# One level of Strassen's scheme for the gate, up and down products of a two-stage fp32 block

## The reference

```python
# stage 0, per batch element b: a dense layer plus a sum over signs
sign = 2 * mask - 1                                  # mask is 0/1, 8 x 1024 x 1024
x = x + (x @ W.T + bias + (x @ sign) * coeff[b])
# stage 1: gated feed-forward layer, F = 2752, with low-rank adapters (rank 16, one of 16 for each b)
gate = x @ W_gate.T + lora(x, A_gate, B_gate)
up   = x @ W_up.T   + lora(x, A_up, B_up)
act  = silu(gate) * up
x = x + (act @ W_down.T + lora(act, A_down, B_down))
# lora(v, A, B) = ((v @ A[i].T) @ B[i].T) * 0.5
```

## Time and profile before

| | |
|---|---|
| median of 3 runs | 1733.05 us (1732.14 to 1736.02) |
| span of the profiled execution | 1731.7 us; what lies around it is not recorded, the median is 1.35 us above it |
| busy: PE, VectorE, ScalarE, POOL | 98%, 49%, 36%, 5% |
| matmuls | 8192 |
| moved by DMA | 216.86 MB, mean 125 GB/s |

### The profile page before, as it was taken

The page is one execution under the profiler, slowest core; times in us unless marked ns, Lnnn a source line. Parts: engine busy times, 40 slices in busy tenths (PEclk is TensorE's granted clock), DMA queues, the critical chain, the costliest instruction groups (busy, mean ns, idle before and its releaser), DMA issues.

```text
span 1731.7 us, 23473 instructions
## 1 busy us (share of the span) xinstructions
PE 1702.4 (98%) x8192; PEld 1437.0 (83%) x8192; DVE 841.2 (49%) x1178; ACT 631.8 (36%) x938; POOL 80.2 (5%) x158
## 2 busy tenths in 40 slices
PE   7899999999999999999999999999999999999998
PEld 7788888888988888888897888888889788888887
DVE  8644334336954334433784433443478443333335
ACT  7433233235733223322663322332366332232222
POOL 1001001001000100100100010010010001000000
PEclk9999999999999999999999999999999999999999
DMA  8625234325742423423573242342366324223222
GB/s 306 175 85 127 90 115 122 99 86 154 245 136 90 130 88 114 124 97 102 171 234 118 88 127 85 121 119 97 96 197 222 110 87 123 97 86 107 90 71 77
DMA packets 66212, 216.86 MB, mean 125 GB/s; under 512 B 9360, under 2 KB 9488, under 8 KB 66128
## 3 DMA queue, kind: packets, MB, share of 16 engines
q1 hardware_dynamic: 54704, 188.97, 34.3%
q0 software_dynamic: 6816, 18.49, 4.9%
q10 hardware_dynamic: 4608, 8.39, 1.3%
HBM read 207.43 MB, written 8.39 MB: 125 GB/s over the span
## 4 chain that ended last, share of the span: by engine, by line
PE 95%; DMA 2%; DVE 1%; issue 1%; ACT 1%; SPq 0%; ACTq 0%; DVEq 0%
PE gate_ps L900 12%; PE gate_ps L904 12%; PE gate_ps L901 12%; PE up_ps L904 9%; PE up_ps L900 9%; PE up_ps L901 9%; PE down_ps L900 9%; PE down_ps L901 9%; PE down_ps L904 9%; DMA raw<-in_mask 2%; PE up_ps L903 1%; PE gate_ps L903 1%; PE td_ps L1008 1%; PE td_ps L1010 1%; PE ta_ps L952 1%
## 5 line engine op out<-in xcount | busy, mean ns | idle before, releaser
L631 DVE TENSOR_TENSOR lo<-raw,hi 128x1024 fp32r<-128x1024 f32 (+2 forms) x368 | 403.1, 1096 | 54.6 <-ACT hi L376 49.9
L376 ACT ACTIVATE hi<-raw 128x1024 fp32r<-128x1024 f32 (+1 forms) x336 | 342.5, 1019 | 218.7 <-PE down_ps L904 152.9
L900 PE MATMUL down_ps<-acth,hi 128*128 128x512 f32 x672 | 262.2, 390 | 0.3 <-DVE stage L634 0.3
L904 PE MATMUL gate_ps<-x1h,lo 128*128 128x512 f32 x672 | 262.3, 390 | 0.0
L904 PE MATMUL up_ps<-x1h,lo 128*128 128x512 f32 x672 | 262.3, 390 | 0.0
L900 PE MATMUL up_ps<-x1h,hi 128*128 128x512 f32 x672 | 262.0, 390 | 0.0
L900 PE MATMUL gate_ps<-x1h,hi 128*128 128x512 f32 x672 | 261.9, 390 | 0.0
L901 PE MATMUL down_ps<-actl,hi 128*128 128x512 f32 x672 | 261.9, 390 | 0.0
L901 PE MATMUL up_ps<-x1l,hi 128*128 128x512 f32 x672 | 261.8, 390 | 0.0
L901 PE MATMUL gate_ps<-x1l,hi 128*128 128x512 f32 x672 | 261.8, 390 | 0.0
L904 PE MATMUL down_ps<-acth,lo 128*128 128x512 f32 x672 | 261.6, 389 | 0.0
(11 more groups left out here) (92 smaller groups left out, 1959.8 us busy)
## 6 DMA issues: line engine op xcount, KB each, us to landing
raw<-in_wgu SPq DMA_DIRECT2D x168, 512.0 KB, 3.3
raw<-in_mask SPq DMA_DIRECT2D x64, 512.0 KB, 3.6
raw<-in_wd SPq DMA_DIRECT2D x64, 512.0 KB, 3.7
w_in<-in_w SPq DMA_DIRECT2D x32, 512.0 KB, 4.9
raw<-in_wd SPq DMA_DIRECT2D x32, 384.0 KB, 4.1
out<-stage ACTq DMA_DIRECT2D x32, 256.0 KB, 2.5
b_in<-in_b_gu POOLq DMA_DIRECT2D x48, 128.0 KB, 5.3
x_in<-in_x POOLq DMA_DIRECT2D x24, 256.0 KB, 2.9
```

The source lines that it names most:

```text
L376: return nc.scalar.activation(o, i, ACT.Copy)
L631: return nc.vector.tensor_tensor(o, a, b, ALU.subtract)
L900: mm(dst, hi[:, u, w], vh, start=first, stop=False)
L904: end = mm(dst, lo[:, u, w], vh, start=False, stop=last)
```

## The change

Each of the three large products A B is cut into quarters and done by Winograd's form of Strassen's scheme: 7 products of quarter size for 8, at the price of sums of quarters ahead of and behind them. The quarters of A are weight tiles (for gate and up, the rows of the two matrices are paired so that a11 and a12 belong to the gate and a21 and a22 to the up matrix, as the host lays them out; for down, they are pairs of output tiles), the columns of B are two halves of 512 tokens each, and the inner dimension is halved.

- The batch is worked in two blocks s of 1024 tokens (four elements), each in two halves of 512 columns.
- Stage 0 is done for the whole batch first: 64 chunks in a row. x1 is written to DRAM (`x1_scratch`) by POOL.
- For each s, x1 is read back through six buffers `fx`, the sums t1 to t4 of its quarters are made (`form_make`) and seven operands of four k tiles each are split and kept in SBUF (`op_b`). The order of reading, making and splitting is the list `FORM`; the first pair of tiles is done in the order of `FIRST_PRODUCTS` while the operands form, with the adapter products `ta` in between.
- For each of 21 pairs of gate and up tiles: four weight quarters of 128 x 512 are loaded, four sums s1 to s4 made (`make_first`, `make_second`), seven tiles split, seven products p1 to p7 made in three PSUM banks. Later products go on in the bank of earlier ones, so ScalarE or VectorE first takes out what the bank holds (`copied`, `c_made`). The half-filled last pair uses four products (`FUSED`).
- The activations are split, their sums t1 to t4 made, split too and stored in DRAM (`operand_scratch`) as seven operands for each pair of feature tiles, 512 KB each, by POOL.
- Down runs in 5 segments of two k pairs; the 14 operand tiles of a segment (7.34 MB) are read back by POOL (`load_operand`) into one of two sets in `op_d`; for each of 4 pairs hp of output tiles 7 products of 6 matmuls are made, and VectorE adds each at once to `acc` (`add_down`), which starts as x1 read back from DRAM. The last one and a half feature tiles of down (`left`) are done as before.
- The loops are unrolled: every engine has straight code, and one counter (`pe_done`) tells how far TensorE has got.

The core of the diff (the lines that go are those of the functions printed above):

```diff
-BLOCKS, PAIR = 4, 2
-T = PAIR * S
+BLOCKS, HALVES = 2, 2
+N = HALVES * S
...
+PRODUCTS = ["p1", "p5", "p6", "p3", "p7", "p2", "p4"]
+FIRST_PRODUCTS = ["p1", "p2", "p5", "p6", "p3", "p7", "p4"]
+FUSED = ["q1", "q2", "q3", "q4"]
+WEIGHT = {"p1": "a11", "p5": "s1", "p6": "s2", "p3": "s4", "p7": "s3", "p2": "a12", "p4": "a22",
+          "q1": "a11", "q2": "a12", "q3": "sum", "q4": "neg"}
...
+MOVING = {"p1": "b11", "p5": "t1", "p6": "t2", "p3": "b22", "p7": "t3", "p2": "b21", "p4": "t4",
+          "q1": "b11", "q2": "b21", "q3": "b22", "q4": "t2"}
...
+def pe_order():
+    order = [("s", m) for m in range(2 * len(first_stage_order()))]
+    for s in range(BLOCKS):
+        order += [("g", s, 0, "p1"), ("g", s, 0, "p2")] + [("ta", s, k) for k in range(KQ)]
+        order += [("g", s, 0, "p5")] + [("ta", s, k) for k in range(KQ, HT)]
+        order += [("g", s, 0, u) for u in FIRST_PRODUCTS[3:]]
+        for f in range(1, PAIRS):
+            order += [("g", s, f, u) for u in PRODUCTS[:4]] + [("td", s, f - 1)]
+            order += [("g", s, f, u) for u in PRODUCTS[4:]]
+        order += [("g", s, PAIRS, u) for u in FUSED[:2]] + [("td", s, PAIRS - 1)]
+        order += [("g", s, PAIRS, u) for u in FUSED[2:]]
+        for seg in range(SEGS):
+            for hp in range(HP):
+                order += [("d", s, seg, hp, u) for u in PRODUCTS]
+                if seg == 0 and hp == 0:
+                    order += [("td", s, PAIRS)]
+        order += [("l", s, h) for h in range(HT)]
+    return order
...
+    x1_d = nc.dram_tensor("x1_scratch", (BLOCKS, HT, HALVES, P, N), f32, kind="Internal").ap()
+    ops_d = nc.dram_tensor("operand_scratch", (BLOCKS, KP, 7, P, 2 * N), f32r, kind="Internal").ap()
+    a20_d = nc.dram_tensor("act_scratch", (BLOCKS, HALVES, P, 2 * N), f32r, kind="Internal").ap()
...
+        FORM = ([("b11", k) for k in range(KQ)] + [("b21", k) for k in range(KQ)] + [("t1", k) for k in range(KQ)]
+                + [(n, k) for k in range(KQ) for n in ("b22", "t3", "t2", "t4")])
...
+            def fx_dma(s, name):
+                n = fx_index[s, name]
+                if n >= FX_RING:
+                    old_s, old = fx_list[n - FX_RING]
+                    if old[0] == "t1b":
+                        sp.wait_ge(form_t, form_t_count(old_s, "t1", old[1]))
+                    else:
+                        sp.wait_ge(form_l, form_count(old_s, *old))
+                o, h = next((o, h) for e, o, h in fx_loads if e == name)
+                sp.dma_start(fx_ap(s, name), x1_d[s, o, h, :, :]).then_inc(fx_loaded[n % FX_RING], 16)
...
+            def load_operand(s, seg, u):
+                name = MOVING[u]
+                for kp in range(SEGK):
+                    at_op = opd_at(seg, name, kp, 0)
+                    pool.dma_start(op_d[:, at_op:at_op + 2, :].rearrange("p a n -> p (a n)"),
+                                   ops_d[s, seg * SEGK + kp, STORED[name], :, :]
+                                   ).then_inc(opd_loaded[opd_sem(seg, name, kp)], 16)
...
+                for i, count in enumerate(stores_upto((s, KP, "b11"))):
+                    pool.wait_ge(ot_stored[i], 16 * count)
+                pool.wait_ge(pe_done, done["g", s, PAIRS - 1, "p4"])
+                for u in PRODUCTS[:4]:
+                    load_operand(s, 0, u)
+                pool.wait_ge(a21_l, HALVES * (s + 1))
+                load_acc(s, 0)
+                load_acc(s, 1)
+                pool.wait_ge(pe_done, done["g", s, PAIRS, "q4"])
+                for u in PRODUCTS[4:]:
+                    load_operand(s, 0, u)
+                for h in range(2, HT):
+                    load_acc(s, h)
+                for half in range(HALVES):
+                    pool.dma_start(a20[:, 2 * half:2 * half + 2, :].rearrange("p a n -> p (a n)"), a20_d[s, half, :, :]
+                                   ).then_inc(a20_loaded, 16)
+                for u in PRODUCTS:
+                    load_operand(s, 1, u)
...
+                for seg in range(2, SEGS):
+                    for u in PRODUCTS:
+                        pool.wait_ge(pe_done, done["d", s, seg - 2, HP - 1, u])
+                        load_operand(s, seg, u)
+                pool.wait_ge(pe_done, done["d", s, SEGS - 2, HP - 1, PRODUCTS[-1]])
...
+            def form_make(s, name, k):
+                def loaded(e):
+                    n = fx_index[s, (e, k)]
+                    dve.wait_ge(fx_loaded[n % FX_RING], 16 * (n // FX_RING + 1))
+                loaded(name)
+                own_ap = fx_ap(s, (name, k))
+                if name == "t1":
+                    loaded("t1b")
+                    end = sub(own_ap, own_ap, fx_ap(s, ("t1b", k)))
+                elif name == "t3":
+                    loaded("b22")
+                    end = sub(own_ap, fx_ap(s, ("b22", k)), own_ap)
+                elif name == "t2":
+                    dve.wait_ge(form_t, form_t_count(s, "t3", k))
+                    end = add(own_ap, fx_ap(s, ("t3", k)), own_ap)
+                else:
+                    dve.wait_ge(form_t, form_t_count(s, "t2", k))
+                    end = sub(own_ap, own_ap, fx_ap(s, ("t2", k)))
+                end.then_inc(form_t, 1)
+            def form_lo(s, name, k):
+                dve.wait_ge(form_h, form_count(s, name, k))
+                sub(op_b[:, op_at(name, k, 1), :], fx_ap(s, (name, k)), op_b[:, op_at(name, k, 0), :]
+                    ).then_inc(form_l, 1)
...
+            def make_second(g):
+                dve.wait_ge(s_made, plan.made[g, "s3"])
+                dve.wait_ge(lo_ready, at[(*g, "p1")] + 1)
+                sub(raw_ap(g, "a11"), raw_ap(g, "s1"), raw_ap(g, "a11")).then_inc(s_made, 1)
+                dve.wait_ge(s_made, plan.made[g, "s2"])
+                if plan.entry_after[g, "s4"]:
+                    dve.wait_ge(lo_ready, plan.entry_after[g, "s4"])
+                sub(raw_ap(g, "s4"), raw_in(g, "a12"), raw_ap(g, "a11")).then_inc(s_made, 1)
...
+                elif u == "p3":
+                    dve.wait_ge(pe_done, done[key])
+                    dve.wait_ge(copied, copy_count(s, f, "p6"))
+                    if f:
+                        dve.wait_ge(a_made, a_count(s, f - 1, 0))
+                    else:
+                        dve.wait_ge(t_ready, 4 * (s + 1))
+                    add(g2[:, :], u2c[:, :], y_ps[:, :]).then_inc(c_made, 1)
+                elif u == "p7":
+                    dve.wait_ge(pe_done, done[key])
+                    dve.wait_ge(copied, copy_count(s, f, "p5"))
+                    add(u2[:, :], x_ps[:, :], p5c[:, :]).then_inc(c_made, 1)
+                    dve.wait_ge(silu_made, silu_count(s, f, 1))
+                    dve.wait_ge(c_made, c_count(s, f, "c22"))
+                    if f > 1 and f % 2 == 0:
+                        dve.wait_ge(ot_l, ot_index[s, kp - 1, "t3"] + 1)
+                    mult(a32[:, 1 + f % 2, :], g2[:, :], u2[:, :]).then_inc(a_made, 1)
+                    if f > 1 and f % 2 == 0:
+                        for name, src in (("t2", t_sum[:, :]), ("t4", a32[:, 0, :])):
+                            operand_lo((s, kp - 1, name), src)
+                elif u == ("p2" if f else "p4"):
+                    dve.wait_ge(pe_done, done[key])
+                    dve.wait_ge(copied, copy_count(s, f, "p1"))
+                    add(g1[:, :], p1c[:, :], z_ps[:, :]).then_inc(c_made, 1)
+                    operand_lo((s, kp, ("b12", "b22")[f % 2]), a32[:, 1 + f % 2, :])
+                if u == "p4":
+                    dve.wait_ge(pe_done, done[key])
+                    dve.wait_ge(silu_made, silu_count(s, f, 0))
+                    dve.wait_ge(c_made, c_count(s, f, "c11"))
+                    if f % 2:
+                        dve.wait_ge(tm, tm_count(s, kp, "t1"))
+                    elif f:
+                        dve.wait_ge(ot_l, ot_index[s, kp - 1, "t4"] + 1)
+                    mult(a32[:, 0, :], g1[:, :], x_ps[:, :]).then_inc(a_made, 1)
+                    operand_lo((s, kp, ("b11", "b21")[f % 2]), a32[:, 0, :])
+                    dve.wait_ge(a_made, a_count(s, f, 0))
+                    if f % 2:
+                        dve.wait_ge(ot_l, ot_index[s, kp, "b21"] + 1)
+                        sub(a32[:, 1, :], a32[:, 2, :], a32[:, 1, :]).then_inc(tm, 1)
+                        sub(t_sum[:, :], a32[:, 2, :], t_sum[:, :]).then_inc(tm, 1)
+                        dve.wait_ge(tm, tm_count(s, kp, "t2"))
+                        sub(a32[:, 0, :], a32[:, 0, :], t_sum[:, :]).then_inc(tm, 1)
+                    elif f < PAIRS - 1:
+                        sub(t_sum[:, :], a32[:, 1, :], a32[:, 0, :]).then_inc(tm, 1)
+                    lora_b(s, f + 1)
...
+            def add_down(key):
+                _, s, seg, hp, u = key
+                g = (s * SEGS + seg) * HP + hp
+                x_ps, y_ps, z_ps = ps[3 * (g % 2)], ps[3 * (g % 2) + 1], ps[3 * (g % 2) + 2]
+                bank = {"p5": y_ps, "p3": y_ps, "p2": z_ps}.get(u, x_ps)
```

(99 more changed lines are left out.)

1735 lines of the change are left out of this document (943 added, 792 removed).

## The result

Median 1717.6 us (1715.0 to 1718.8, four runs) against 1733.9 of the kernel before (1732.1 to 1736.0, four runs): ratio 0.9904, 95% interval 0.9892 to 0.9915, 1.0% faster. The forecast was 1673 us, 3.5% faster. The saving of matmul work came as counted; the new stops cost 44 us more than my sum.

A forecast was written before the change was run, and what follows sets the result against it. TensorE, busy 1702.4 of 1731.7 us, was taken to bound the kernel. After the change 1534.1 us of matmul work plus 138 us of stalls gave a 1672 us span, so 1673 us measured; forecast 1650 to 1695, wider range 1630 to 1722.

The forecast's parts named there:

- Work saved: Whole kernel: PE work falls by 156.1 us to 1534.1 us, with 7502 matmuls left.
- Stage 0: 64 chunks in a row at the start: 4 us lost (bounds 0 and 15).
- four signs of being wrong: Gate pairs over 21.7 us; down group over 11; op_d landing over 40 after issue; stage 0 ending past 215.
- Operands and first pair: First gate and up pair of each half, operands formed from x1: 62 us lost together (bounds 30 and 90).
- Start of down: Start of down, twice: PE waits for operands being loaded, 24 us for both (bounds 10 and 50).
- Down, steady: the coupling: Steady down: products wait for late VectorE adds, 0.5 us in each of 40 groups, 20 us (bounds 0 and 60).
- End: End of the kernel: two adds, issue and a 512 KB store, 5.5 us.
- paced by adds or clock: Rival, 1713 us, chance 0.17: down groups lose 1.5 us instead of 0.5, or slower-clock matmuls after stops cost 43.
- Slower through POOL's queue: Rival, 1765 us, chance 0.1: in down the operands come too slowly through POOL's queue.
- Better hidden: Rival, 1631 us, chance 0.18: neighbouring k reads overlap (62 becomes 42), slack in down absorbs late adds (20 becomes 0).

The follow-up runs named there:

- the reordered kernel: Changed kernel with six edits together (x reads, adapter tiles, low halves, down adapter, start of down, last stores): 1678.6 us, 0.9695 of the kernel before.
- the filler: Changed kernel plus 56 matmuls in each half that compute nothing for the result, put into PE's stops while operands form: 1721.7 us.

## Why the prediction was wrong
- **Work saved** (156 us): right. 7502 matmuls at 0.228 us in both steady stages.
- **Stage 0** (4 us, measured 17): mis-sized. I compared VectorE's time and the DMA rate with PE's and never followed one read of x: issued two chunks ahead, behind a mask and often W, 6.2 us to land, with ScalarE in order behind it. Issuing it earlier got back 9 of the 13 us of excess. Of the four signs of being wrong this one came: stage 0 ended at 217, past 215.
- **Operands and first pair** (62, measured 80): the chain and the price of its steps k were right; mis-sized by 18 was what comes ahead of the adapter product. In the first half it starts at 26.7 instead of 21: p2 starts at 14.9 where I had b21 done at 12.5, and the adapter product 11.9 us after p2, where I had 8.5 from b21 to t1. In the second half I took 6 us off the first because the adapter matrices were there, and it came 1.5 earlier only: p1 itself started 8.1 us after the last product of down against 4.6, because VectorE was still 6 us behind PE with its adds, the sums and low halves of the next weights. What the reads in this stretch cost apart from their order no run shows.
- **Start of down** (24, measured 37): the first group was right. The last operand was there 33.6 us after p4 of the last whole pair, where I had 31.6, and up to the group's end 12.1 and 11.9 us were lost, where I had 12. Missing was a second stop, 6.5 us a half and with what belongs to it the other 13: the down adapter's hand-overs between ScalarE and VectorE, queued ahead of the add of p6's result, for which p7 waits. I had priced the moved work and not asked what stands behind it. Spreading it gave 13 us back.
- **Down, steady: the coupling** (20, measured 7.5, of which 3.9 lie right behind the second stop): wrong, and the one large term in my favour. I added up lateness from whole durations; VectorE was 86% busy (138 of 160 us) and PE never stopped in that window. Neighbouring operations overlap, and the add starts on time. Without this error the forecast would have been 12 us further off, so that much of its nearness is luck.
- **End** (5.5, measured 15.8): the store's landing was nearly right, 6.6 us after the last matmul. Missing was POOL's DRAIN of 8.65 us after it, exposed by a queue that was not used for the last stores before.
- **Rivals.** The number of *paced by adds or clock* (1713) is the nearest. Its first mechanism, paced groups, did not happen. Its second did in part: by the timeline some 200 matmuls start at about twice the usual step, 35 us in all against 8 in the kernel before, nearly the 43 that it names. But most of them lie in stretches that wait for reads, VectorE or ScalarE anyway, and the filler gave nothing back; only those right behind the second stop of down, 3.9 us, are seen to be lost. *Slower through POOL's queue* is out: from 722 to 745 POOL's queue moved 8.44 MB, 367 GB/s, where its row before gave 218 for small pieces. *Better hidden* was right in one half, the slack in down took in the late adds, and wrong in the other, the reads of neighbouring k did not overlap (the steps took the 5 us of the serial chain). That the reordered kernel comes near the forecast says nothing for the forecast, since its gains are at other places than I had named.

In short: the matmul count fixes the gain, and the stage borders cost half as much again as I gave them (start and stage 0, operands, start of down and end: 166 us for 112), of which the rest of down gave 12 back. What stays open is what POOL's DRAIN waits for, and how much of the 80 us of operand forming a different placement in memory could hide; neither was tried.

## What to carry to other kernels
Price a restructured kernel by its borders: at each one follow the first transfer, the engine queue that it sits in and everything behind the waiting instruction, for a small hand-over placed ahead of a needed add costs as much as a late megabyte. A stage whose mean load is 86% on the helping engine can run without a stop, so a latency sum over single operations is not evidence of a loss. Before an order is changed, look whether DMA is full in that window: where it was at 272 GB/s earlier issue paid 9 us, where it was near 400 it paid at most 3. And compare edits by the stage that they touch: unedited stages differed by 2 us and more from trace to trace.
